# Three attention loops: tiles written out, first pass three groups ahead, loads re-ordered

## The reference

```python
def expert_step(acc, params):
    q = (x @ qw.T + qb_).reshape(B, S, H, Dh).transpose(0, 2, 1, 3)
    k = (x @ kw.T + kb_).reshape(B, S, H, Dh).transpose(0, 2, 1, 3)
    v = (x @ vw.T + vb_).reshape(B, S, H, Dh).transpose(0, 2, 1, 3)
    p = jax.nn.softmax(jnp.einsum('bhqd,bhkd->bhqk', q, k) * scale, axis=-1)
    o = jnp.einsum('bhqk,bhkd->bhqd', p, v)
    o = o.transpose(0, 2, 1, 3).reshape(B, S, E) @ ow.T + ob_
    return (acc + o * g[..., None], None)
```

## Time and profile before

| | us |
|---|---|
| median of 3 runs | 4910.73 |
| lowest, highest run | 4908.14, 4930.1 |
| profiled execution | 4940.64 |
| its span | 4939.0 |
| instructions in it (a number) | 142944 |
| PE, DVE, ACT, POOL busy | 3549.6, 3202.2, 2588.6, 700.0 |
| first attention loop, about | 151 to 871 |
| causal attention loop, about | 1040 to 1486 |
| routed attention loop, about | 2769 to 4724 |

### The profile page before, as it was taken

How to read it: one execution, slowest core, us unless ns; L and a number is a source line. 1 busy time by engine, 2 the same in 40 slices (tenths; PEclk the granted TensorE clock), 3 DMA queues, 4 the chain that set the end, 5 groups by cost and what they waited for, 6 DMA issues and landing times. The chain is left out here.

```text
span 4939.0 us, 142944 instructions
## 1 busy us (share of the span) xinstructions
PE 3549.6 (72%) x55309; PEld 2015.0 (41%) x55309; DVE 3202.2 (65%) x3717; ACT 2588.6 (52%) x4898; POOL 700.0 (14%) x1500
## 2 busy tenths in 40 slices
PE   1699999259998965557533288887888887888838
PEld 0355555125556732224422144444444444444414
DVE  2689889338862149984522377777777776777744
ACT  1478888127783432212111167676677666666632
POOL 0000000011000007850300011111111111111120
PEclk6799999669998977778666589898889898888868
DMA  3000000200000012200333444444444444444410
GB/s 53 18 9 8 7 8 8 38 28 13 8 5 18 17 72 86 102 18 4 37 105 109 99 91 94 94 95 89 93 92 98 86 96 87 94 89 94 94 44 21
DMA packets 173983, 286.61 MB, mean 58 GB/s; under 512 B 94796, under 2 KB 139538, under 8 KB 149134
## 3 DMA queue, kind: packets, MB, share of 16 engines
q1 hardware_dynamic: 168670, 272.05, 24.0%
q0 software_dynamic: 4656, 5.18, 0.5%
HBM read 220.57 MB, written 41.52 MB: 53 GB/s over the span
## 5 line engine op out<-in xcount | busy, mean ns | idle before, releaser
L825 ACT ACTIVATE channels_qk<-psum 128x512 f32<-128x512 f32 (+1 forms) x3908 | 2108.7, 592 | 822.6 <-PE psum L693 515.7
L887 DVE TENSOR_REDUCE l2f_chunk_max<-psum 128x2 f32<-128x1024 f32 x1168 | 1386.5, 1223 | 517.1 <-PE psum L666 510.4
L887 DVE TENSOR_REDUCE chunk_max<-psum 128x2 f32<-128x1024 f32 (+2 forms) x848 | 946.6, 1161 | 150.5 <-PE psum L666 110.6
L714 PE MATMUL psum<-channels_qk,l2f_v_and_ones 128*9 128x128 f32 x18448 | 779.7, 292 | 7.0 <-ACT channels_qk L825 5.5
L693 PE MATMUL psum<-l2f_q_parts,l2f_k_parts 51*128 51x128 bf16 x9224 | 495.5, 231 | 245.3 <-ACT channels_qk L825 116.3
L666 PE MATMUL psum<-l2f_k_parts,l2f_q_parts 48*128 48x512 bf16 x2336 | 491.1, 417 | 90.6 <-issue 69.3
L666 PE MATMUL psum<-k_parts,q_parts 48*128 48x512 bf16 (+3 forms) x1696 | 328.4, 390 | 270.4 <-DMA q_parts<-q_parts_dram 226.2
L714 PE MATMUL psum<-channels_qk,v_and_ones 128*9 128x128 f32 x12560 | 505.2, 281 | 0.1
L693 PEld LDWEIGHTS psum<-l2f_q_parts,l2f_k_parts 51*128 51x128 bf16 x9224 | 301.0, 100 | 490.8 <-ACT channels_qk L825 328.0
L714 PEld LDWEIGHTS psum<-channels_qk,l2f_v_and_ones 128*9 128x9 f32 x18448 | 417.4, 94 | 144.9 <-issue 34.2
L693 PE MATMUL psum<-q_parts,k_parts 51*128 51x128 bf16 x6280 | 324.8, 223 | 44.7 <-ACT channels_qk L825 15.1
(11 more groups left out here) (478 smaller groups left out, 3564.0 us busy)
## 6 DMA issues: line engine op xcount, KB each, us to landing
l2f_k_parts<-l2f_k_parts_dram SPq DMA_DIRECT2D x298, 192.0 KB
l2f_v_and_ones<-expert_v_dram SPq DMA_DIRECT2D x37, 1152.0 KB, 6.6
l2f_k_parts<-l2f_k_parts_dram SPq DMA_DIRECT2D x298, 128.0 KB
l2f_k_parts<-l2f_k_parts_dram SPq DMA_DIRECT2D x298, 64.0 KB
l1a_bc_rows<-ssm_rows_dram SPq DMA_DIRECT2D x16, 1024.0 KB, 5.4
expert_v_dram<-l2f_v_and_ones SPq DMA_DIRECT2D x8, 1152.0 KB
channels_qk<-ssm_rows_dram SPq DMA_DIRECT2D x8, 1024.0 KB
expert_q_dram<-heads_out SPq DMA_DIRECT2D x8, 1024.0 KB, 9.3
```

The costliest lines, as they stand in the source:

```text
L714: last = nc.tensor.matmul(oT[32 * m:32 * m + HD + 1, g * P:(g + 1) * P], vx(k)[:, kt, 4 * g + m, :], at.prob[:, s % 4, j, kk, pp * P:(pp + ...
L825: nc.scalar.activation(at.prob[:, s % 4, j, 0:kts, :].rearrange("p k q -> p (k q)"), c.ps[:, ring.bank(i, n), 0:kts * 2 * P], ACT.Exp, sca ...
L887: v.tensor_reduce(at.mx[:, 4 * g + 2 * pp:4 * g + 2 * pp + 2, chunk], c.ps[:, 2 * (n % 2):2 * (n % 2) + 2, 0:span.width(tile, chunk)], X, ...
```

## The change

- All three loops are written out tile by tile. In the routed one the 32 tiles that are always there stand without a condition; the rest are four pairs, each in a conditional of its own. The number of rounds is read after the 32nd tile.
- The first pass is three groups ahead in the first and in the routed attention: group 0 of the next tile is first-passed from step 8 on. Rows are turned 13 steps before they are read. Three query buffers in all loops (one was there unused), with two semaphores.
- Routed side work: "q" at step 12, "outT" at 14, "proj" at 20; all but "q" are left out of tile 0. GpSimd gathers before its first split of a tile, and splits queries before the maxima in group 2.
- SyncE's order in the routed loop: six key DMAs after the rows of every group (group 3 of the next tile, then groups 0, 1, 2 of the tile after next), the values in two halves (in groups 1 and 2), and the twelve query loads at the end, for the tile after next, ahead of the store of the output. Three groups of keys and the queries of tile 1 are loaded ahead of tile 0.
- The first pass for a seventeenth tile of the first attention is left out. One more tile of the routed output is blanked.

```diff
+        if i > 0 and s == min(4, 4 * steps - 2):
+            names.append("out")
+        if self.routed and s == 12:
+            names.append("q")
+        if self.routed and i > 0 and s in (14, 20):
+            names.append("outT" if s == 14 else "proj")
...
-    SLOTS = 2 if tri is None else 3
+    SLOTS = 3
...
     def each_tile(eng, body):
-        if tri is not None:
+        if not routed:
             for i in range(tiles):
-                body(i, i % 2, i // 2)
-            return tiles // 2
-        if not routed:
-            with eng.Fori(0, tiles // 2) as r:
-                for k in range(2):
-                    body(r * 2 + k, k, r)
-            return tiles // 2
+                body(i)
+            return tiles
+        for i in range(2 * routed.least_rounds):
+            body(i)
         rounds = eng.value_load(routed.rounds[0:1, 0:1], min_val=routed.least_rounds, max_val=tiles // 2)
-        with eng.Fori(0, tiles // 2) as r:
-            with eng.If(r < rounds):
-                for k in range(2):
-                    body(r * 2 + k, k, r)
-        return rounds
+        for r in range(routed.least_rounds, tiles // 2):
+            with eng.If(rounds > r):
+                body(2 * r)
+                body(2 * r + 1)
+        return rounds * 2
...
-            def routed_loads(i, k, r):
+            def routed_loads(i):
                 this, following, e = expert(i), expert(i + 1), expert(i + 2)
                 for g in range(G):
-                    load_later_max(i, g, k)
+                    load_later_max(i, g)
                     if g == 0:
-                        load_q(1 - k, i + 1)
-                        load_keys(c, at, sp, 1 - k, following, 1, k_loaded[1 - k][1])
-                    elif g == 1:
-                        load_keys(c, at, sp, 1 - k, following, 2, k_loaded[1 - k][2])
-                    elif g == 2:
+                        load_group(i + 1, 3, following)
+                    else:
+                        load_group(i + 2, g - 1, e)
+                    if g == 1 or g == 2:
                         sp.wait_ge(pv_done, span.step_base(i) + 4)
-                        load_values(1 - k, following)
-                    else:
-                        load_keys(c, at, sp, 1 - k, following, 3, k_loaded[1 - k][3])
-                        sp.wait_ge(s2_read, ring.read_when(i, ring.place(i, "proj")))
-                        store_y(i, y_stored)
-                        load_w_out(this)
-                        load_keys(c, at, sp, k, e, 0, k_loaded[k][0])
+                        load_values(i + 1, g - 1, following)
+                    if g == 3:
+                        load_q(i + 2)
+                        if i > 0:
+                            sp.wait_ge(s2_read, ring.read_when(i, ring.place(i, "proj")))
+                            sp.dma_start(routed.y_dram[i], routed.y[:, :]).then_inc(y_stored, 16)
+                            load_w_out(this)
...
                 for g in range(1, G):
-                    load_keys(c, at, sp, 0, first, g, k_loaded[0][g])
+                    load_group(0, g, first)
                 load_w_out(first)
-                load_values(0, first)
-                load_keys(c, at, sp, 1, second, 0, k_loaded[1][0])
-            elif tri is not None:
-                load_q(1, 1)
+                for half in range(2):
+                    load_values(0, half, first)
+                for g in range(G - 1):
+                    load_group(1, g, second)
+            load_q(1)
...
                 for g in range(G):
-                    group, tile, _, _ = first_pass_of(i, g, k, r)
+                    group, tile = first_pass_of(i, g)
                     if routed and g == 0:
                         pool.wait_ge(routed.list_loaded, i * 16 + 48)
+                        routed.gather(pool, i % 2)
+                    if routed and g == 2:
+                        pool.wait_ge(q_loaded[(i + 1) % 2], ((i + 1) // 2 + 1) * QL)
+                        pool.wait_ge(s2_read, ring.read_when(i, ring.place(i, "q")))
+                        split_q()
                     if exists(tile):
-                        split_max(group, tile, tile_link)
-                    if routed and g == 0:
-                        routed.gather(pool, k)
...
-            v.memset(at.prob[:, 3, :, :, :], 1.0).then_inc(s2_read, ring.BANKS)
...
-        attention_loop(c, at, 2)
+        attention_loop(c, at, 3)
...
-        attention_loop(c, at, 2, routed=rt)
+        attention_loop(c, at, 3, routed=rt)
...
+                pool.dma_start(rt.y_dram[0], blank_y[:, :]).then_inc(y_blanked, 16)
```

More of the change, by code:

```diff
@@ L322, with __init__ @@
     BANK0, BANKS = 4, 3
-    def __init__(self, span, lead, routed):
+    def __init__(self, span, lead, tiles, routed):
         self.span, self.lead, self.late = span, lead, 2 if span.causal else 1
[L326 to L330, removed]
-        else:
-            self.size = len(self.fills(0))
-            assert self.size % self.BANKS == 0
+        self.tiles, self.routed = tiles, routed
+        self.orders = [self.fills(i) for i in range(tiles + 1)]
+        self.base = [self.BANKS if routed else 0]
+        for order in self.orders:
+            self.base.append(self.base[-1] + len(order))
+        self.size = len(self.orders[1])
+        assert not routed or self.base[1] == self.size and self.size % self.BANKS == 0
     def rows_in(self, g):
@@ new lines, in turn_heads, with project @@
+            def turn_heads(i, n):
+                pe.wait_ge(s2_read, ring.free_when(i, n))
+                pe.wait_ge(heads_ready, i + 1)
+                nc.tensor.transpose(c.ps[:, ring.bank(i, n), 0:P], c.heads[:, 0, :], c.ident[:, :]).then_inc(s2_ready, 1)
+            def project(i, n, turned):
+                pe.wait_ge(s2_read, ring.free_when(i, n))
+                pe.wait_ge(s2_read, ring.read_when(i, turned))
+                pe.wait_ge(w_out_loaded, i * 16)
+                nc.tensor.matmul(c.ps[:, ring.bank(i, n), 0:P], routed.outT[:, :], routed.w_out_now[:, :], start=True, stop=True).then_inc(s2_ready, 1)
@@ L736, in fill, with side_work @@
+            def side_work(i, g, name):
+                n = ring.place(i, name)
                 if name == "out":
[L737 to L740 removed]
+                    turn_out(i, n)
                 elif name == "outT":
[L742 removed]
@@ L820, in probabilities @@
             def probabilities(s, j, i, n):
[L821 removed]
+                kts = len(span.key_tiles(i, s % span.steps(0 if routed else i)))
                 act.wait_ge(s2_ready, ring.number(i, n + 1))
@@ L872, in _ @@
             copy_out_channels(done)
-            empty("out", done, 0 if tri is not None else 2)
+            empty("out", done, ring.place(tiles, "out"))
             if routed:
```

336 lines of the change are left out of this document (150 added, 186 removed).

## The result

The changed kernel takes **4685.13 us** (median of four, 4677.88 to 4696.37), the kernel before in the same comparison 4911.6: ratio **0.9534** (95%: 0.9503 to 0.9564). It is faster, by 226 us; 386 were predicted, and 4685 lies above the range's 4640.

What follows compares the result with a forecast made beforehand. The routed loop was taken to lose time to waits at jumps and for rows of maxima; -373 + 7 + 12 + 3 - 35 = -386 gave 4555 us from the profiled 4940.6, or 4525 against the median, range 4485 to 4640.

Steps and rivals of the forecast that it cites:

- What a clean tile takes: Tile time without stalls, from group times: 42.5 us in the routed loop, 40.5 in the first attention.
- the eight maxima ahead: First attention: maxima ahead of its first tile cost 9.1 us, turning a gain of 44 into the term -35.
- Written-out tiles: Routed loop: seventeen jumps go; with the waits gone, 36 tiles fall from 52.86 to 42.5 us each, -373.
- both kinds of wait: Routed loop: ScalarE waiting for issue, 182.1 us in 35 waits; TensorE waiting for rows of maxima, 108.6 in 52.
- rival 4: Routed straight code must be loaded: 208 packets, each stalling TensorE 5.2 us, would give 5605 us; chance 0.03.
- a matter of SyncE's order: Routed tile: rows of maxima issue behind twelve query and six key loads, so TensorE waits 2.49 us.
- a jump costs 9.3: Routed loop: a tile with the jump takes 57.5 us, one inside a pair 48.2, so a jump costs 9.3.
- the 5.7 us given to the late rows: Routed tile: the present stall for rows of maxima costs 48.2 - 42.5 = 5.7 us a tile.
- rival 3: Routed loop: traffic, not SyncE's order, makes rows late; only the jumps go, about 4731 us; chance 0.05.
- Routed start: Before the first routed tile: two more key groups and the second query stand ahead of rows, +12 us, bounds 9.1 to 21.
- Remaining conditionals and end: Routed loop: conditionals falling through and small stalls, +7 us (0 to 21); query loads ahead of the last store, +3 (0 to 9).
- Rivals 1 and 2: Routed loop: queries late at step 8 (margin 3.0 us, chance 0.12); gather late at step 12 (6.6, 0.10); 4730 us each.

Runs made afterwards that it cites:

- e1_light: Changed kernel with each routed key load cut to one row and each half of the values to one partition, same issues and semaphores; ratio 0.9135.
- e13: Kernel before (hardware loops) with three more 720 KB device-memory copies a tile on SyncE's queue; ratio 1.013.
- e14: Kernel before with one 8 KB row in each routed key load, the second tile's keys loaded once ahead of the loop; ratio 0.9488.
- e7: Changed kernel with one-row key loads and, in their place, four 720 KB device-memory copies a tile; ratio 0.9242.
- e12: Changed kernel loading only on a change of expert (0.917), first two rows of maxima issued ahead of second tile's keys and queries; ratio 0.9255.

## Why the prediction missed

*What a clean tile takes*: right. 42.5 predicted, 42.2 in e1_light; 40.5 for the first attention, 40.1 measured, and that part's -35 was -43.7: the eight maxima ahead cost 5.6 (225.78 - 179.63 less a tile of 40.5), not 9.1, fourteen tiles were 0.27 us shorter each, and the last interval was 37.7 and not 39.3.

*Written-out tiles, "with both kinds of wait gone each tile takes 42.5 us"*: this step failed. Both kinds went, as said, but rival 4's mechanism took 101 us in their place, in 63 waits instead of 208, of 1.6 us each instead of 5.2, and the lower clock after them the rest: 36 x (46.2 - 42.5) = 133 us, as much as the whole miss of 129 in the profiled span. Rival 4 was put at 0.03 because "straight stretches show no issue wait". They were loop bodies, which e13 shows to be nearly immune, and written-out tiles of the causal attention, whose DMA engines are idle (share 0.01). The case that mattered, code run once under a share of 0.56, was in no row. The bound should have been read as an unknown cost at 0 to 5.2 us each, added to the sum, not as a rival of all or nothing. The Trainium skill ("Runtime: NRT & Kernel Launch", section on instruction fetch mechanics) calls the fetch of code in sequence hidden and has a stall only for a taken branch outside the loaded pages. Here it is contradicted: 79 us of stalls in 1380 us of written-out code, and 51 of the 53 end just behind a packet of the instruction queue.

*What bounds the kernel: "a matter of SyncE's order", a jump costs 9.3*: half right. e14 keeps order and jumps and takes the traffic of the keys away: the waits for rows vanish, and a jump costs about 6.4. The late rows needed the traffic, the jump only in part. The 9.3 was itself too low as a reading: before the change, too, the lower clock behind a jump reached into the next tile (0.51 from 3132.1 to 3139.9, behind the copy of 3132.1 in the tile with the jump), so part of the 5.7 us given to the late rows belonged to the jump. The sum takes both together and is not touched. So rival 3 (the traffic, not the order) had more in it than its 0.05, though the lead of three groups did remove the late rows.

*Routed start*: +12 predicted, +24.5 in the table, but the term itself was right. From the loop's first matmul to the first of the second pass it took 30.05 us (2782.02 to 2812.07) and takes 42.86 now (2745.99 to 2788.85): +12.8. The loads in front are what the rows wait for, as said; they show as query issues that held SyncE for 22.27 us, where 8.7 us were taken, and for the upper bound only. Of the other 11.7 us, 7.7 lie ahead of that first matmul: from the last copy of the first attention it is 1919.3 us away, 1911.6 before, and in the versions that leave everything ahead of it alone 1904 to 1922, so this is within the scatter of single profiles. The last 4 are a slow first tile.

*Remaining conditionals and end*: the end of the loop is one 8.6 us issue wait and a last tile of 55.5 us; in e1_light it is 49.7, 7.5 above its mean. So +7 was right by luck: it was argued for branches not taken around the tiles that run, and what cost was the jump over the pairs that don't run.

*The range*: its lower end is 4495 by its own terms, not 4490, and 4525 + 103 is 4628, not 4640. Neither matters beside 4685.

*Rivals 1 and 2*: absent. No TensorE wait for query parts or gathered queries in the loop; the margins of 3.0 and 6.6 us held.

## What to carry to other kernels

Writing a loop out trades a jump's stall for a program that has to arrive in time all along, and in this kernel that needed DMA engines with time to spare: it was free below a busy share of 0.2, cost 21 us in 1380 at 0.36 and 79 at 0.56. Before unrolling a stage that streams operands, look at its DMA share, and at whether the streamed data is already there: loading keys and values only when the expert changes was worth 3 to 4%, and taking the key traffic from the old loop gave 5%, as much as the whole change. When a stall has two explanations in the profile, an order and a traffic, take the traffic away in one run before pricing either.

## What the chip showed that was not expected

- Straight code stalls for its own program: 51 of 53 stalls end 1.2 to 1.8 us after a 16 KB packet of the instruction queue has landed, and the packet starts late rather than taking long.
- The stalls follow the engines' busy share and not the bytes: 112 GB/s in e7 cost 21 us, 105 in the changed kernel 79.
- Packets of 4 KB and 2 KB in place of 8 KB did not help: 92 and 103 us against 79 and 86.
- Code in a loop, though loaded anew in each round by the size of the instruction queue, stalls at its jump but hardly between (11 us at a share of 0.54 against 74 written out).
- The profile can name a wait for a DMA "issue": the 15.95 us at the start went when the rows of maxima were issued earlier (e12), and no packet of the instruction queue landed in the 12 us before they ended. "Issue" is therefore not always an instruction that wasn't there yet.
